# A gated recurrent block with a mixture of experts on one Trainium2 core: rows sorted by expert through DRAM instead of all experts for all rows

## The chip, the cores and the metric

One core of one Trainium2 chip. Its engines work in parallel and meet at semaphores: TensorE (PE; PEld is its weight load), VectorE (DVE), ScalarE (ACT), GpSimd (POOL) and SyncE (SP), which here only issues DMAs. Each engine takes its instructions in program order. The metric is the device time of one execution in microseconds, the median of several runs.

## What is computed

```
x : (32, 128, 256)  ->  batch 32, 128 time steps, 256 features
step t: r = decay*r + c_t*c_t;  inp = (q_t*r) @ Wi.T + bi;  gate = sigmoid(inp @ Wg.T + bg)     # q = layernorm(x), c = ctx
        blended = gate*state + (1-gate)*inp;  state = tanh(blended @ A.T + inp @ Bm.T);  out_t = state @ Wo.T + bo
x = x + tanh(g_xattn) * out
f = layernorm(x)                                       # 4096 rows of 256
shared = swiglu(f @ w_shared_in) @ w_shared_out;  hid = swiglu(f @ w1_shared)
probs = softmax(f @ w_gate + gate_bias)                # 8 experts
routed = sum over the 2 most probable experts e of probs[e] * (hid @ w2[e])
x = x + tanh(g_ffn) * (shared + routed)
```

## The kernel before

**Tiles.** A tile is 8 time steps of the 32 sequences: 256 rows, in two halves of 128. There are 16. A float32 product is made of three fp16 (or fp32r) products of high and low parts: high x high, low x high, high x low. ScalarE makes the high part, GpSimd or VectorE the low one (helper `low`, L1482 on GpSimd).

**The recurrence.** Its 128 steps are a chain: `gated_state` on VectorE forms (1 + gate) x state as u_hi (L1077) and u_lo (L1079, L1082); `recurrence` on TensorE multiplies (8 small matmuls L484, 4 small ones L489) into the tile's accumulator `rec`, which already holds the products that don't depend on the state; `tanh_step` on ScalarE (L777) gives the new state.

**Iterations.** Every engine has a function `iteration(i)`, for i = 1 to 18. Iteration i does the 8 steps of tile i, and between them, as fillers in a fixed order, stages of other tiles: of a = i + 1 the input products (inp, gate, bm, a), of c = i - 1 the output product Wo, second layernorm, w_shared_in, router logits and w1, of d = i - 2 the hidden layers and expert products, of e = i - 3 the last expert products, and of f = i + 2 the first layernorm. Iterations 3 to 12 run in a loop of two; tile 0 and the preparation of weights stand ahead. What stands between step k and k + 1 is called slot k below. Because the engines keep their order, whatever waits in a slot holds the next step up.

**Expert products.** All 8 experts are computed for all rows: `pair(n, m)` multiplies one half of tile m with two experts at once, 6 matmuls of 512 columns (L470):

```python
for kc in range(KC):
    for a, part in ((a_hi, 0), (a_hi, 1), (a_lo, 0)):
        last = pe.matmul(dst, a[:, kc, s * P:(s + 1) * P], w(part, kc), start=first, stop=(kc == KC - 1 and a is a_lo), ...)
```

and `add_pair` on VectorE adds the two results, each times its column of weights `wts` (0 where the expert isn't chosen):

```python
dve.scalar_tensor_tensor(out=o, in0=bank[B_PAIR[n]][:, 0:D], scalar=wts[m % 2][:, s, 2 * q:2 * q + 1], in1=o, op0=ALU.mult, op1=ALU.add)   # L1095
dve.scalar_tensor_tensor(out=o, in0=bank[B_PAIR[n]][:, D:2 * D], scalar=wts[m % 2][:, s, 2 * q + 1:2 * q + 2], in1=o, ...)                  # L1098
```

There are 8 pairs a tile, in slots 0, 1, 2 (of tile e) and 3, 4, 5 (three in slot 5; of tile d). The router's logits come out of TensorE transposed and are turned on VectorE (L1453); which two experts are chosen is found by comparing all with all: `more` and `same` on VectorE (L1352, L1353), five small passes on GpSimd (L1563 to L1580).

**The other fillers of TensorE**: slot 0 transposes of xn1 (L516); slot 1 Wo; slot 2 the shared output product (so); slot 3 inp and gate; slot 4 bm, transposes of xn2 (L528); slot 6 w_shared_in (sh) and logits (L747); slot 7 a and both halves of w1.

**The second layernorm** is a chain through four engines: `projected` (L1167), statistics (L1369 to L1389) on VectorE in slot 2, power and product on GpSimd (L1587, L1589), xn on ScalarE (L860), which stands between the tanh of step 3 and that of step 4; then TensorE transposes. The first layernorm (`x_rstd` on GpSimd, xn1 L849 on ScalarE) stands between the tanh of steps 6 and 7, `residual` (L1498) follows on GpSimd.

**Order of the DMA queue.** SyncE issues per iteration the loads of x, context and the residual's x, and the output of tile i - 3.

## Time and profile before

| | |
|---|---|
| median of 3 runs (531.85 to 532.77) | 532.03 us |
| profiled execution, its own time | 534.36 us |
| its span, first to last instruction | 532.1 us |
| mean granted TensorE clock | 0.973 |
| PE busy | 494.0 us, 93% |
| DVE busy | 436.9 us, 82% |
| ACT busy | 216.6 us, 41% |
| POOL busy | 174.8 us, 33% |

Times below are of that execution, from its span's start. Matmuls are pipelined: "busy" counts each from issue to a modelled end, so how fast TensorE goes is read from distances between starts. The granted clock is a share of full speed, 2.4 GHz.

### The profile page before, as it was taken

How to read it: one execution, taken by the hardware profiler on the slowest of the kernel's cores; microseconds unless marked ns; L12 is line 12 of the kernel's file. 1: busy time of each engine (PE TensorE's matmuls, PEld its weight loads, DVE VectorE, ACT ScalarE, POOL GpSimd, SP SyncE). 2: the span in 40 equal slices, each digit the busy share in tenths (PEclk: the TensorE clock that was granted, in tenths of full speed). 3: DMA queues.
4: the chain of work that ended last, by engine and by line, in shares of the span. 5: the costliest groups of instructions: out<-in, count | busy, mean ns of one | idle time of the engine just before them, and what ended most of it. 6: DMA issues, size and time to landing. Idle time of an engine off the chain costs nothing.

```text
span 532.1 us, 12569 instructions
## 1 busy us (share of the span) xinstructions
PE 494.0 (93%) x4506; PEld 369.6 (69%) x4506; DVE 436.9 (82%) x1382; ACT 216.6 (41%) x500; POOL 174.8 (33%) x261
## 2 busy tenths in 40 slices
PE   5978677999999999999999999999999999979986
PEld 4865566776867776767768777767678687747552
DVE  3788849788898978888898989888888978797976
ACT  4566564443533434434434335344444343322120
POOL 3021564432324233233323243332433243241330
PEclk8999788999999999999999999999999999989999
DMA  6751011020202020110202020301220101000001
GB/s 158 228 165 35 1 36 26 2 61 22 60 22 59 10 69 0 47 32 20 59 20 59 20 59 0 73 5 36 43 59 1 41 1 42 1 20 1 22 1 39
DMA packets 46062, 22.05 MB, mean 41 GB/s; under 512 B 35664, under 2 KB 39376, under 8 KB 46032
## 3 DMA queue, kind: packets, MB, share of 16 engines
q1 hardware_dynamic: 45904, 21.65, 15.8%
q8 instruction: 18, 0.29, 0.2%
q0 software_dynamic: 128, 0.00, 0.1%
q14 instruction: 12, 0.10, 0.1%
HBM read 17.45 MB, written 4.19 MB: 41 GB/s over the span
## 4 chain that ended last, share of the span: by engine, by line
PE 59%; DVE 23%; issue 6%; ACT 5%; POOL 1%; DVEq 0%; ACTq 0%
PE bank L459 22%; PE bank L470 21%; PE rec L459 8%; DVE r L1115 3%; PE rec L484 3%; ACT c L788 3%; DVE x L1167 2%; DVE acc L1095 2%; DVE u_full L1079 2%; PE rec L489 2%; DVE c_turned L1108 2%; DVE u_hi L1077 2%; PE bank L528 1%; PE bank L747 1%; DVE ret L1128 1%
## 5 line engine op out<-in xcount | busy, mean ns | idle before, releaser
L777 ACT ACTIVATE state<-rec 128x64 f32<-128x64 f32 x128 | 36.7, 286 | 177.8 <-PE rec L489 177.5
L470 PE MATMUL bank<-w_hi,hid_hi 128*128 128x512 f16 x256 | 97.8, 382 | 8.8 <-DVE x L1167 5.0
L470 PE MATMUL bank<-w_hi,hid_lo 128*128 128x512 f16 x256 | 97.8, 382 | 0.0
L470 PE MATMUL bank<-w_lo,hid_hi 128*128 128x512 f16 x256 | 97.7, 382 | 0.0
L1077 DVE SCALAR_TENSOR_TENSOR u_hi<-gt,state 128x64 f16<-128x64 f32 x127 | 36.4, 286 | 52.3 <-ACT state L777 52.0
L1098 DVE SCALAR_TENSOR_TENSOR acc<-bank,wts,acc 128x256 f32<-128x256 f32 x128 | 62.0, 484 | 4.5
L1095 DVE SCALAR_TENSOR_TENSOR acc<-bank,wts,acc 128x256 f32<-128x256 f32 x128 | 60.8, 475 | 1.8 <-PE bank L470 1.6
L484 PE MATMUL rec<-u_hi,a_hi 128*128 128x32 f16 x512 | 47.6, 194 | 10.5 <-DVE u_hi L1077 9.6
L484 PEld LDWEIGHTS rec<-u_hi,a_hi 128*128 128x128 f16 x512 | 38.0, 98 | 24.8 <-DVE u_hi L1077 18.5
L1482 POOL TENSOR_TENSOR cn_lo<-cn,cn_hi 128x512 fp32r<-128x512 f32 x14 | 17.9, 1276 | 102.4 <-ACT cn_hi L840 102.4
L470 PEld LDWEIGHTS bank<-w_hi,hid_hi 128*128 128x128 f16 x256 | 25.0, 98 | 33.1 <-DVE x L1167 6.5
L484 PE MATMUL rec<-u_hi,a_lo 128*128 128x32 f16 x512 | 47.3, 193 | 0.0
L470 PEld LDWEIGHTS bank<-w_hi,hid_lo 128*128 128x128 f16 x256 | 25.2, 98 | 30.5 <-issue 0.6
L1079 DVE SCALAR_TENSOR_TENSOR u_full<-gt,state 128x64 f32<-128x64 f32 x127 | 39.7, 312 | 0.0
L470 PEld LDWEIGHTS bank<-w_lo,hid_hi 128*128 128x128 f16 x256 | 25.2, 98 | 20.1 <-issue 0.3
L484 PEld LDWEIGHTS rec<-u_hi,a_lo 128*128 128x128 f16 x512 | 35.1, 98 | 5.7 <-issue 0.3
L1082 DVE TENSOR_TENSOR u_lo<-u_full,u_hi 128x64 f16<-128x64 f32 x127 | 35.3, 278 | 4.4
L1482 POOL TENSOR_TENSOR hs_lo<-hs,hs_hi 128x512 f16<-128x512 f32 x16 | 18.6, 1164 | 60.7 <-ACT hs_hi L961 60.7
L489 PE MATMUL rec<-u_lo,a_hi 128*128 128x32 f16 x512 | 36.3, 194 | 2.3 <-DVE u_lo L1082 1.5
L1482 POOL TENSOR_TENSOR st_lo<-state,st_hi 128x512 f16<-128x512 f32 x16 | 18.6, 1161 | 55.8 <-ACT st_hi L949 55.8
L860 ACT ACTIVATE xn<-x,nr,rs 128x256 f32<-128x256 f32 x32 | 17.5, 594 | 47.0 <-POOL nr L1589 47.0
L459 PE MATMUL bank<-xn_hi,sh_hi 128*128 128x256 f16 x128 | 35.6, 278 | 0.0
(228 smaller groups left out, 1460.9 us busy)
## 6 DMA issues: line engine op xcount, KB each, us to landing
x_sb<-in_x_dram SPq DMA_DIRECT2D x16, 256.0 KB, 3.2
c_sb<-in_ctx_dram SPq DMA_DIRECT2D x64, 64.0 KB, 2.8
xr_sb<-in_x_dram SPq DMA_DIRECT2D x16, 256.0 KB, 3.3
out_dram<-acc SPq DMA_DIRECT2D x16, 256.0 KB, 2.5
raw_w<-in_L_ffn_w_dram SPq DMA_DIRECT2D x8, 256.0 KB, 4.4
raw_sh<-n_L_ffn_w_shared_in_dram SPq DMA_DIRECT2D x1, 512.0 KB, 6.2
raw_w<-in_L_ffn_w_shared_dram SPq DMA_DIRECT2D x1, 512.0 KB, 6.6
raw_Wi<-in_L_xattn_Wi_dram SPq DMA_DIRECT2D x1, 256.0 KB, 3.3
```

The source lines that it names most:

```text
L459: last = pe.matmul(o, w[:, kc, at], a[:, kc, :], start=first, stop=(kc == KC - 1 and w is w_lo), skip_group_check=True)
L470: last = pe.matmul(dst, a[:, kc, s * P:(s + 1) * P], w(part, kc), start=first, stop=(kc == KC - 1 and a is a_lo), skip_group_check=True)
L484: pe.matmul(o[:, oc, :], w[:, kc, oc * P:(oc + 1) * P], u_hi[t % 2][:, kc, :], start=False, stop=False, skip_group_check=True)
L489: last = pe.matmul(o[:, oc, :], a16[0][:, kc, oc * P:(oc + 1) * P], u_lo[t % 2][:, kc, :], start=False, stop=(kc == KC - 1), skip_group_ch ...
L777: act.activation(step_of(state[i % 2], t), step_of(rec[i % 2], t), ACT.Tanh, scale=1.0 / PSCALE).then_inc(st_ready[t], 1)
L860: last = act.activation(xn2[c % 2][:, s, :], x1[c % 2][:, s, :], ACT.Identity, bias=nr2[c % 2][:, s:s + 1], scale=rs2[c % 2][:, s:s + 1])
L1077: dve.scalar_tensor_tensor(out=u_hi[p][:, :, :], in0=gate, scalar=1.0, in1=old, op0=ALU.add, op1=ALU.mult).then_inc(uh_ready[t_next], 1)
L1079: dve.scalar_tensor_tensor(out=u_full[p][:, :, :], in0=gate, scalar=1.0, in1=old, op0=ALU.add, op1=ALU.mult).then_inc(uf_ready, 1)
L1082: dve.tensor_tensor(u_lo[p][:, :, :], u_full[p][:, :, :], u_hi[p][:, :, :], ALU.subtract).then_inc(ul_ready[t_next], 1)
L1095: dve.scalar_tensor_tensor(out=o, in0=bank[B_PAIR[n]][:, 0:D], scalar=wts[m % 2][:, s, 2 * q:2 * q + 1], in1=o, op0=ALU.mult, op1=ALU.add) ...
L1098: dve.scalar_tensor_tensor(out=o, in0=bank[B_PAIR[n]][:, D:2 * D], scalar=wts[m % 2][:, s, 2 * q + 1:2 * q + 2], in1=o, op0=ALU.mult, op1= ...
L1482: pool.tensor_tensor(n, whole, hi, ALU.subtract).then_inc(signal, 1)
```

## The change

Tiles 0 to 14 no longer multiply all experts. They are taken in groups ("chunks") of four, four, four and three tiles. For a group:

1. Each tile's hid goes as rows of 512 fp16 (high and low part) into `hid_rows`, because w1 is now computed with rows on the partitions (`w1_part`; half of w1 moves from slot 7 to slot 0 of the next iteration).
2. VectorE finds the two chosen experts with `max` and `max_index`, and one-hot rows of them. TensorE sums them over the group's rows (`prefix`), VectorE works out from it where each row goes (`places`, `rows`): rows of an expert stand together, each expert from a multiple of 128 on, and a table says which expert a block of 128 rows has.
3. GpSimd scatters the rows to DRAM (`hrows`) by indexed DMAs, 4 a tile of 128 rows each.
4. SyncE reads two blocks at a time back, transposed by the DMA (`turn_rows`), into a ring of four buffers. A group has at most 23 blocks (19 for the last): 12, 12, 12 and 10 "duos".
5. `duo` on TensorE multiplies a duo's blocks, each with its expert, whose number it reads from the table into a register: 12 matmuls of 256 columns. ScalarE copies the result to SBUF, SyncE stores it to DRAM (`yrows`).
6. GpSimd gathers, 4 indexed DMAs a tile, the two result rows of each row, and VectorE adds them with their weights (`combine_first`, `combine_second`) into `acc`, of which there is now one per tile.

Duos stand in slots 2, 4 and 5, one each, from iteration last tile of the group + 4 on: iterations 7 to 15 have three, iteration 16 has nine in slot 5 (after the transposes of tile 15), iteration 17 has the last group's ten in slot 5. Scatters stand in the iterations 5 and 6, 9 and 10, 13 and 14, 16; gathers in 11, 12, 15, 16, 17, 18; combines in 12 to 18. Tile 15 stays dense: its eight pairs come after the last duo. Both DRAM buffers of rows are filled with zeros at the start, by two DMAs that ScalarE issues. The loop is written out. The context's transpose and the scan run for tile i + 2 instead of i + 1. The logits product has 8 small matmuls with rows on the partitions, so that VectorE's four transposes and the comparisons go, with GpSimd's five passes.

The core of the diff (lines that rename semaphores and tiles are left out):

```diff
+CHUNKS = ((0, 4), (4, 4), (8, 4), (12, 3))
+DENSE = 15
+RING = 4
+def blocks_of(q):
+    return 4 * CHUNKS[q][1] + E - 1
...
+            def turn_rows(n):
+                q, j, blocks = duo_chunk(n)
+                if j == 0:
+                    sp.wait_ge(scattered, 16 * 4 * (last_of(q) + 1))
...
+                    sp.wait_ge(duo_done, n - RING + 1)
+                sp.dma_start_transpose(hid_t[n % RING][:, :, 0:blocks * P],
+                                       hrows[q % 2][2 * P * j:2 * P * j + blocks * P, :]).then_inc(ht_in[n % RING], 16)
+            def store_y(n):
...
+                sp.wait_ge(y_ready, n + 1)
+                sp.dma_start(yrows[q % 2][2 * P * j:2 * P * j + blocks * P, :].rearrange("(b p) d -> p b d", p=P),
+                             y_sb[n % RING].rearrange("p (b d) -> p b d", d=D)[:, 0:blocks, :]).then_inc(y_out[n % RING], 16)
...
+                for slot in range(STEPS):
+                    for n in DUOS.get((i, slot), ()):
+                        store_y(n)
+                        if n + RING < duos_before(duo_chunk(n)[0] + 1):
+                            turn_rows(n + RING)
+                for q in range(len(CHUNKS)):
+                    if i == START[q] - 1:
+                        for n in range(RING):
+                            turn_rows(duos_before(q) + n)
...
+            def duo(n, dst):
+                q, j, blocks = duo_chunk(n)
+                pe.wait_ge(ht_in[n % RING], 16 * (n // RING + 1))
+                first = True
+                for b in range(blocks):
+                    at = 2 * j + b
+                    e = pe.value_load(table[q][0:1, at:at + 1], min_val=0, max_val=E - 1)
+                    for kc in range(KC):
+                        for part, half in ((0, 0), (1, 0), (0, 1)):
+                            last = pe.matmul(dst[:, b * D:(b + 1) * D], hid_t[n % RING][:, half * KC + kc, b * P:(b + 1) * P],
+                                             split["w2"][part][:, kc, bass.ds(e, 1), :].rearrange("p a b -> p (a b)"), ...)
+            def prefix(q):
+                n = 2 * CHUNKS[q][1]
+                pe.wait_ge(hot_ready, last_of(q) + 1)
+                for pick in range(2):
+                    pe.matmul(dst[:, 0:n * E], upper[:, :], hots[q][:, :, pick, :], ...)
+                for g in range(n):
+                    for pick in range(2):
+                        last = pe.matmul(dst[:, (g + 1) * E:(n + 1) * E], ones16[:, :], hots[q][:, g, pick, :]..., ...)
...
             def iteration(i, k):     # TensorE
-                    pair(5, e, k)
+                    w1_part(d, D, bank[B_W1B], w1_done, k)
                 recurrence(i, 1, k)
-                    pair(6, e, k)
                 recurrence(i, 2, k)
-                    pair(7, e, k)
+                duos_at(i, 2)
+                for q in range(len(CHUNKS)):
+                    if d == last_of(q):
+                        prefix(q)
                 recurrence(i, 3, k)
-                    pair(0, d, k)
                 recurrence(i, 4, k)
-                    addend_bm(a, k)
-                    pair(1, d, k)
+                duos_at(i, 4)
                     x1_transposed(c, k)
                 recurrence(i, 5, k)
-                    pair(2, d, k)
-                    pair(3, d, k)
-                    pair(4, d, k)
+                    addend_bm(a, k)
+                duos_at(i, 5)
+                if i == DENSE + 2:
+                    for n in range(E):
+                        pair(n)
...
+            for n in range(2):       # ScalarE, setup
+                act.dma_start(hrows[n].rearrange("(b p) d -> p b d", p=P),
+                              zeros[:, :].unsqueeze(1).to_broadcast([P, MOST_BLOCKS, 2 * D])).then_inc(zeroed, 16)
+            def y_evacuated(i, slot):    # ScalarE, after tanh 3, 5 and 6
+                    act.wait_ge(duo_done, n + 1)
+                    act.copy(y_sb[n % RING][:, cols], duo_bank(n, i, slot)[:, cols]).then_inc(y_ready, 1)
...
+            def combine_first(t):
+                dve.wait_ge(gathered[t % 4], 64 * (t // 4 + 1))
+                for s in range(HALVES):
+                    last = dve.scalar_tensor_tensor(out=acc[t][:, s, :], in0=yg[t % 4][:, s, 0, :], scalar=mix[:, t, s, 0:1],
+                                                    in1=acc[t][:, s, :], op0=ALU.mult, op1=ALU.add)
+            def places(q):           # VectorE, slot 4 of iteration last tile + 2; seven small operations
+            def rows(q):             # VectorE, slot 5 of it; six more, the last:
+                dve.tensor_copy(slots_i[q][:, :], slots_f[:, 0:2 * n]).then_inc(routed, 1)
...
+            def scatter(t, s, pick):
+                    pool.wait_ge(routed, 5 * (q + 1))
+                pool.indirect_dma_start(hrows[q % 2], bass.IndirectOffsetOnAxis(ap=slots_i[q][:, at:at + 1], axis=0),
+                                        hid_rows[t % 6][:, s, :, :].rearrange("p a d -> p (a d)"), None, ...).then_inc(scattered, 16)
+            def gather(t, s, pick):
+                    for r in range(RING):
+                        pool.wait_ge(y_out[r], 16 * IN_RING[q][r])
+                    pool.wait_ge(combined, t - 3)
+                pool.indirect_dma_start(yg[t % 4][:, s, pick, :], None, yrows[q % 2], bass.IndirectOffsetOnAxis(...), ...)
+            for q, (t, n) in enumerate(CHUNKS):
+                r = last_of(q) + 2
+                if r < TILES:
+                    spread(SCATTERS, r, range(t, t + 2), [5] * 4 + [7] * 4)
+                    spread(SCATTERS, r + 1, range(t + 2, t + n), range(8))
+                else:
+                    spread(SCATTERS, r, range(t, t + n), [5] * 4 + [6] * 4 + [7] * 4)
...
                 # GpSimd's iteration: moves(i, 0) to moves(i, 7) issue what is planned for (i, spot)
+                moves(i, 0)          # after st_lo
                 low(hs_s[1], ...)
+                moves(i, 1)
                 low(hid_rows[d % 6][:, :, 1, :], ...)
+                moves(i, 2)
                 # second layernorm's power and product
+                moves(i, 3)
+                moves(i, 4)
                     cn_low(a, k)
+                moves(i, 5)
                 x_rstd(f, k)
+                moves(i, 6)
                 residual(i, k)
+                moves(i, 7)
```

## Rows read from the trace of the kernel before

**Rows 1.** Stretches: length, busy us (xcount) of PE, PEld, DVE, ACT, POOL, clock, DMA share.
```profile
0.00:51.86 51.86, 38.97 (x303) 32.95 (x304) 36.14 (x114) 29.02 (x60) 10.43 (x20) 0.90 0.55 150
51.86:81.60 29.74, 22.17 (x216) 18.30 (x215) 20.79 (x65) 17.95 (x38) 16.30 (x18) 0.83 0.13 28
81.60:111.30 29.70, 27.13 (x259) 21.46 (x260) 24.47 (x77) 12.00 (x29) 13.36 (x18) 0.94 0.13 28
...
170.16:434.85 264.69, 260.23 (x2486) 196.29 (x2487) 227.91 (x738) 109.08 (x261) 89.25 (x135) 1.00 0.14 33
...
464.24:487.78 23.54, 20.87 (x190) 13.35 (x189) 18.52 (x60) 5.29 (x15) 6.51 (x11) 0.93 0.03 12
487.78:532.10 44.32, 37.92 (x230) 21.92 (x228) 34.46 (x91) 7.83 (x15) 10.13 (x17) 0.98 0.05 19
```
**Rows 2.** Timeline of ScalarE, the tanh of steps 3 to 6 of one tile.
```profile
237.59 0.29 ACT L777 ACTIVATE state<-rec 128x64 f32<-128x64 f32 x1 [0.77 <-PE rec L489]
...
242.64 0.29 ACT L777 ACTIVATE state<-rec 128x64 f32<-128x64 f32 x1 [0.50 <-PE rec L489]
...
246.25 0.28 ACT L777 ACTIVATE state<-rec 128x64 f32<-128x64 f32 x1 [1.88 <-PE rec L489]
250.48 0.29 ACT L777 ACTIVATE state<-rec 128x64 f32<-128x64 f32 x1 [1.79 <-PE rec L489]
```
**Rows 3.** The chain of waits, 216.8 to 246.3: start, us, what.
```profile
216.81 3.88 PE bank L470 x18
...
221.05 2.62 PE bank L459 x24
...
224.11 0.23 PE rec L484 x8
224.34 0.12 PE rec L489 x4
224.46 1.49 PE rec L459 x12
...
239.42 2.81 PE bank L459 x24
```
**Rows 4.** VectorE by line and form.
```profile
L1095 DVE SCALAR_TENSOR_TENSOR acc<-bank,wts,acc 128x256 f32<-128x256 f32 x128 | 60.8, 475 | 1.8 <-PE bank L470 1.6
...
L1453 DVE STREAM_TRANSPOSE lg_t<-bank 32x64 f32<-32x64 f32 x64 | 15.6, 244 | 2.6 <-PE bank L747 2.0
```
**Rows 5.** Timelines of VectorE and ScalarE: first use of w2, and one layernorm.
```profile
42.60 1.86 DVE L1049 TENSOR_REDUCE w2max<-raw_w 128x1 f32<-128x512 f32 x3
...
236.50 0.26 DVE L1077 SCALAR_TENSOR_TENSOR u_hi<-gt,state 128x64 f16<-128x64 f32 x1
...
239.70 0.16 DVE L1389 TENSOR_SCALAR nm<-mv 128x2 f32<-128x2 f32 x1
...
241.05 1.09 ACT L860 ACTIVATE xn<-x,nr,rs 128x256 f32<-128x256 f32 x2 [3.17 <-POOL nr L1589]
```
**Rows 6.** DMA queues, and issues with KB each and median us to landing.
```profile
q1 hardware_dynamic: 45904, 21.65, 15.8%
...
out_dram<-acc SPq DMA_DIRECT2D x16, 256.0 KB, 2.5
raw_w<-in_L_ffn_w_dram SPq DMA_DIRECT2D x8, 256.0 KB, 4.4
...
raw_so<-_L_ffn_w_shared_out_dram SPq DMA_DIRECT2D x1, 256.0 KB, 6.9
...
cols<-in_L_xattn_bi_dram POOLq DMA_DIRECT2D x1, 1.0 KB, 2.9
```
**Rows 7.** GpSimd by line: a DMA that it issues.
```profile
L1515 POOL DMA_DIRECT2D cols<-in_L_xattn_bi_dram x1 | 0.8, 781 | 0.0
```
**Rows 8.** The tail: ScalarE's timeline, and the chain of waits.
```profile
497.67 1.09 ACT L860 ACTIVATE xn<-x,nr,rs 128x256 f32<-128x256 f32 x2 [3.06 <-POOL nr L1589]
...
518.95 9.25 PE bank L470 x42
```

More of the change, by code:

```diff
@@ new lines, in duo_slots, with put @@
+        def duo_slots():
+            plan = {}
+            def put(i, slot, n):
+                plan.setdefault((i, slot), []).extend(n)
+            for q in range(len(CHUNKS)):
+                n = list(range(duos_before(q), duos_before(q + 1)))
+                i = last_of(q) + 4
+                while n and i < TILES:
+                    for slot in (2, 4, 5):
+                        put(i, slot, n[:1])
+                        n = n[1:]
+                    i += 1
+                if n:
+                    put(TILES + (q == len(CHUNKS) - 1), 5, n)
+            return plan
@@ new lines, in rows @@
+            def rows(q):
+                n, base, step = 2 * CHUNKS[q][1], 7 * q, 5 * q
+                blocks = blocks_of(q)
+                dve.wait_ge(routing, base + 7)
+                for pick in range(2):
+                    last = dve.tensor_tensor(placed[:, 0:n, pick, :], hots[q][:, :, pick, :], place[:, 0:n, :], ALU.mult)
+                last.then_inc(routed, 1)
+                dve.tensor_reduce(counted[:, 0:blocks], reached[:, 0:blocks, :], AX_X, ALU.add).then_inc(routed, 1)
+                dve.wait_ge(routed, step + 1)
+                dve.tensor_reduce(slots_f[:, 0:2 * n], placed[:, 0:n, :, :].rearrange("p g k e -> p (g k) e"), AX_X,
+                                  ALU.add).then_inc(routed, 1)
+                dve.wait_ge(routed, step + 2)
+                dve.tensor_scalar(table[q][:, :], counted[:, 0:blocks], float(E - 1), None, ALU.min).then_inc(routed, 1)
+                dve.wait_ge(routed, step + 3)
+                dve.tensor_copy(slots_i[q][:, :], slots_f[:, 0:2 * n]).then_inc(routed, 1)
@@ L1540, in iteration, with moves @@
+            for i, tiles in GATHER.items():
+                spread(GATHERS, i, tiles, list(range(8)) if i < TILES else [0, 0, 1, 1, 2, 2, 3, 3] if i == TILES else [5] * 16)
+            def moves(i, spot):
+                for t, s, pick in SCATTERS.get((i, spot), ()):
+                    scatter(t, s, pick)
+                for t, s, pick in GATHERS.get((i, spot), ()):
+                    gather(t, s, pick)
             def iteration(i, k):
```

638 lines of the change are left out of this document (389 added, 249 removed).

## The prediction

> **What bounds the kernel now.** I read four views. The table by stretches [rows 1] divides the span. The recurrence ends at 487.78: 51.86 us of setup and tile 0, 29.7 us each for tiles 1 and 2, 29.4 us for each tile from 3 to 14, 23.5 us for tile 15, then a tail of 44.3 us. In the middle stretch (nine tiles, 264.69 us) TensorE is busy for 260.23 us, VectorE for 227.91, GpSimd for 89.25, at granted clock 1.00, the 2.4 GHz level. The chain of waits [rows 3] shows TensorE going from one filler to the next: between two steps of the recurrence (8 + 4 small matmuls, 0.23 + 0.12 us) lie 18 expert matmuls of 512 columns (3.88 us, so 0.216 each) or 24 of 256 columns (2.62, so 0.109 each). The tanh rows [rows 2] agree: 246.25 to 250.48 is 4.23 us = 3.88 + 0.35. So a step lasts as long as TensorE's filler in its slot plus 0.35, unless a chain across the engines is longer. One is: 237.59 to 242.64 is 5.05 us, which fillers alone don't make. There ScalarE waits for the second layernorm [rows 5]: 3.17 us idle ahead of xn.
>
> **What is removed.** A tile has 8 pairs x 6 matmuls x 0.216 = 10.4 us of expert work on TensorE, all of it in filler slots, and 16 accumulations of 0.475 us on VectorE (7.6 us) [rows 3, 4]. Both go for tiles 0 to 14.
>
> **What is left, slot by slot, without duos (iterations 3 to 6).** Slot k is what lies between steps k and k + 1. TensorE's filler: transposes 0.44 + half of w1 (12 x 0.109 = 1.31); wo 1.31; so 1.31; inp and gate 24 in 2.8; transposes 0.44; bm 1.5 (12 of fp32r); sh and the now small gate product 2.9; a and the other half of w1 2.8 [rows 3]. With 0.35 each they sum to 17.7 us. VectorE needs 25.3 - 7.6 - 1.0 (four small transposes), plus some 1.2 for max, max_index and one-hot rows, so about 18 us. No engine fills a tile alone, so the longest in each slot counts, and I get 2.2, 2.3 (VectorE), 2.1 (VectorE), 4.3, 1.8, 2.4, 3.5, 3.15. The 4.3 is the layernorm chain: from u_hi at 236.50 to xn's end at 242.14 are 5.64 us, of which some 0.2 for the softmax's small rows leave; the tanh is 1.09 after u_hi, and the next tanh is queued behind xn on ScalarE [rows 2, 5]. The 2.4 and 3.5 are ScalarE waiting for blend, and for GpSimd's statistics. Sum 21.75; the same method gives 28.3 for the tile before, against 29.4, so I add 0.6 for waits it doesn't see: **22.3 us, 7.1 less**, four times: 28. Tile 2 (five pairs leave, 6.5 us) gives 7.
>
> **Duos.** A duo is 12 matmuls of 256 columns, 1.31 us, plus two reads of an expert number from SBUF into a register of TensorE and an address worked out from it. No row shows such a read. Between 0 (hidden under the six matmuls before, 0.65) and 1.1 us each (the layernorm's whole pair of ScalarE operations takes 1.09 [rows 5], nothing small costs more) I take 0.4: 2.1 us. Slots 2, 4 and 5 get one each. Slot 2 grows to 3.8, but what follows then isn't the layernorm chain any more (3.15 for inp and gate), slot 4 to 2.8, slot 5 to 3.9, slot 6 falls to 3.25. Sum 24.5, with waits 25: **4.4 less**, eight times (7 to 14): 35. In tile 15 (23.54 before) three pairs of slots keep their size and the duos replace pairs: 19.5, 4 less.
>
> The Trainium skill (DMA: Bandwidth & Descriptors, Latency and other measured facts) gives a register load of about 600 ns as its floor; by it an exposed duo would be 2.5 us and the nine tiles some 10 us longer in all, if each read were exposed. No row here shows it.
>
> **What the sorting adds to the tiles.** Sixty scatters and sixty gathers are issued on GpSimd. Its plain small DMAs take 0.78 us [rows 7]; an indexed one must read 128 offsets too, so the lower end is 0.78, the upper twice that, 1.6, and I take 1.1, between them. One alone between two passes is hidden by GpSimd's idle time (it is busy 9.9 of 29.4 us a tile). Four in one place are not: in iterations 5, 9 and 13 four scatters stand ahead of x_rstd and wait for the routing table, which comes 1.7 us after step 6; xn1 is 4.4 + 0.9 + 1.09 later, and tanh 7 is queued behind xn1 on ScalarE. That is 4.6 us in iteration 5 and 3.3 in 9 and 13; the thirteen dependent small operations of `places` and `rows` on VectorE add 2 in 5, nothing in the others (TensorE's duo covers them), and the queue behind adds about 1 each: 16 us in all. The first duo of a group (7, 11, 15) waits for the last scatter, a landing and a transpose, about 2 us each: 6. Combines on VectorE stand in slot 7 of 12 to 15: 3.4 us. **Sum 25.** Zeroing writes 2 x 2944 rows of 1 KB, 6.0 MB. The queue's 21.65 MB took 15.8% of 532 us [rows 6], so 23 us of all engines, beside the weight loads. Those of w2, the last, land in 4.4 and are first used at 42.6 [rows 5, 6], and in the first 51.86 us the engines' share is only 0.55 [rows 1], so I take the weights as in time; I count 2 us for two DMA issues in ScalarE's full setup, less 1 for the four transposes. If weights come late it is up to 12.
> What moves without a price: scan and context transpose run a tile further ahead, which only lengthens their slack; the loop of the middle tiles is written out, and neither its border nor code loading shows in the 29.4 us before. SyncE waits for the last scatter of a group in iterations 6, 10, 14 and 16; behind it are queued the next loads of x and context, used one to two tiles later, and xr, used a tile later, so at a landing of 4.4 us [rows 6] they stay covered.
> The recurrence then ends at 487.8 + 1 - 7 - 28 - 35 - 4 + 25 = **440**, so 48 us earlier.
>
> **The tail, counted from there (T).** Before it is 44.3. Now 19 duos of two groups and the dense tile remain. Layernorm and transposes of tile 15: before, xn ends at T + 11 [rows 8]; eight gathers (6.6 of them ahead of it) put it at T + 14. Nine duos at 2.1: T + 33. Shared, router and w1 products 5.5, hid and its halves 2.5: T + 41. Ten duos: T + 62. Behind them eight dense pairs, 10.4 us (42 matmuls took 9.25 [rows 8]): T + 72, at the half clock more. Longer is the other way: last duo, copy and store (0.6, 0.5 to issue, 2.5 to land [rows 6]) T + 65.6; twelve gathers 13.2; landing 2.9 [rows 6]; last combine 1.9; output 2.5: **T + 86**, 42 us more than before. A duo is read through a ring of four: its loop is copy 0.6 + issue 0.5 + landing + duo 2.1, and four duos take 8.4; so it is hidden as long as a transposing DMA lands within 5.2 us. The same 256 KB untransposed lands in 4.4 (median) to 6.9 [rows 6]. I take 4.4 to 5.
>
> Against this stands a page. The Trainium skill (VectorE: DVE Perf Modes, The three transpose paths) gives 1309 ns for a 128x128 two-byte transpose by DMA; a duo holds eight of these, and added up they would be an estimated 10.5 us. That rule speaks against the change; as a mechanism of this kernel it is the second rival. No row here shows a transposing DMA.
>
> **Sum.** 440 + 86 = 526 us of span; the profiled run has 2.3 us around its span of 532.1 (534.36 in all), so 528 against 534.4, or 1.2% less. Against the median 532.03 this is **526 us**.
>
> **Rivals.**
> *Cheaper parts* (0.22): indexed DMAs at 0.78 and duos at 1.6. Tiles: 27 duos x 0.5, 12 scatters x 0.3 and 3 us at the starts of groups, 20 less; tail: 19 duos x 0.3 (the ring then holds them at 1.8) and 12 gathers x 0.3, 9 less: 497 us. For it: the DMA row [rows 7] and the queue of TensorE that runs ahead. Against: each duo has addresses to work out.
> *Slow transposes* (0.22, ends slower): one place, the ring of four. With L from a transposing DMA's issue to its landing, a loop of four duos takes L + 3.2 us once L is above 5.2. Nine duos are two loops and a duo, ten are a first L, two loops and two duos, and the first duo of three groups in the tiles waits L as well. So each us of L above 5.2 costs 2 + 3 + 3 = 8 us: at L = 7 14 more, 540; at L = 10 38 more, 564. It decides from L = 5.9 on. For it: two-byte elements must be placed across partitions, and plain landings go to 6.9 already [rows 6]. Against: the middle of them lies at 4.4, on queues fuller than the tail's. (By the page's 10.5 us the time would be an estimated 568.)
> *Dear indexed DMAs* (0.14, ends slower): at 1.6 us each 0.5 x 12 in the last gathers, 0.5 x 12 in the stalls of 5, 9 and 13, some 3 us at the starts of groups, and the last group's scatters end after its ring is free (4 us): 19 more, 545. It decides from 1.3 us on.
> *Nothing gained in the tiles*: the forecast of 22.3 rests on chains; if all tiles stayed at 29.4 the tail would make it 574. The freed 10.4 us of the engine that bounds speak against it (it shares the 0.14).
>
> **Chances and range.** My forecast, the tiles gain 48 and the tail gives back 42, has 0.42. It is a small difference of two large terms, each off by 5 us easily, so its own range is 515 to 538, of which 0.33 lies below 531, 0.03 within 0.2% of 532 (about what a measurement tells from no change) and 0.06 above. Faster is 0.33 + 0.22 = 0.55, slower 0.06 + 0.22 + 0.14 = 0.42, the same 0.03. A tenth on either side is left out by 492 to 564.
>
> **What would show it.** In the profile after: tanh 0 to tanh 0 of iterations 3 and 4 at 22 us and of 8 or 12 at 25, TensorE's share about 80%; the longest single wait of tanh before step 7 of 5, 9, 13, released by GpSimd; the recurrence's end at 440; the rows of indexed DMAs on GpSimd near 1.1 us; the transposes' landing under 5.2; a tail of 86 us whose chain ends in gathers and combines. It is wrong if those DMAs cost another size, if the clock falls to 1.2 GHz in the tail's gaps, or if the weights are late in the setup.

## The result and the profile after

The changed kernel takes **578.73 us** (median of 4 runs, 576.92 to 582.35) against 532.17 for the kernel before beside it: 1.0875 times as long, 95% interval 1.0834 to 1.0916. I had said 526, with 492 to 564. It is slower, and outside the range. A run that takes over 1.5% more than the shortest run of the same kernel is left out of its median; only e8 below has such runs, two of four.

The profiled run took 576.92 us around a span of 575.04. The same cuts as in [rows 1], by tanh 0 of iterations 1, 2, 3 and 15 and by the last tanh (length, then busy us and count of TensorE, its weight loads, VectorE, ScalarE, GpSimd, then granted clock, DMA share, GB/s):

```profile
0.00:59.14 59.14, 42.24 (x303) 35.73 (x304) 36.95 (x108) 29.09 (x59) 11.15 (x24) 0.91 0.82 238
59.14:88.46 29.32, 19.33 (x209) 15.78 (x209) 20.06 (x65) 18.95 (x40) 16.61 (x17) 0.94 0.07 15
88.46:113.04 24.58, 19.62 (x235) 17.20 (x236) 21.04 (x67) 11.57 (x31) 12.32 (x13) 1.00 0.11 28
113.04:436.35 323.31, 271.32 (x3119) 238.74 (x3118) 244.98 (x842) 149.23 (x367) 171.60 (x182) 0.95 0.38 91
436.35:460.06 23.71, 16.84 (x192) 12.92 (x190) 14.88 (x57) 6.42 (x17) 13.71 (x15) 0.93 0.82 183
460.06:575.04 114.98, 61.55 (x398) 36.93 (x396) 45.30 (x132) 18.03 (x34) 55.22 (x55) 0.79 0.60 158
```

Against before: setup and the first two iterations 88.46 - 81.60 = 6.9 us longer; tiles 2 to 15 take 371.6 in place of 406.2, so 34.6 shorter; the tail takes 115.0 in place of 44.3, so 70.7 longer. Sum +43, which is the difference of the spans (575.0 - 532.1). TensorE's share falls from the 98% of the middle stretch before to 84% here and 54% in the tail: it no longer sets the pace. The granted clock shows the same: 96.5 us of the span at the 1.2 GHz level, 28.8 before, and half of the 96.5 (48.7) lie in the tail.

The other rows of the page and the list of waits that answer to [rows 6, 7]: queues and GpSimd's groups, then what ScalarE's layernorms waited for (total us, times, longest).

```profile
q1 hardware_dynamic: 104432, 44.73, 32.8%
q0 software_dynamic: 5888, 15.74, 9.5%
q10 hardware_dynamic: 5920, 6.03, 3.0%
...
L1818 POOL DMA_INDIRECT yg<-yrows,slots_i x60 | 62.0, 1033 | 32.1 <-issue 16.1
L1805 POOL DMA_INDIRECT hrows<-hid_rows,slots_i x60 | 62.8, 1047 | 21.8 <-issue 18.1
```
```profile
ACT xn L1002 <- POOL nr L1747: 58.5, 15, 9.7
ACT xn L1013 <- POOL nr L1880: 46.7, 16, 8.6
```

An indexed DMA holds GpSimd for 1.04 us, as forecast (1.1), but 0.30 us of "issue" stands between two of them: their pitch is 1.30. GpSimd's timeline in iteration 5, where the longest of these waits lies:

```profile
184.09 0.97 POOL L1805 DMA_INDIRECT hrows<-hid_rows,slots_i  x1 [0.30 <-issue]
185.37 0.97 POOL L1805 DMA_INDIRECT hrows<-hid_rows,slots_i  x1 [0.30 <-issue]
186.36 0.74 POOL L1745 TENSOR_TENSOR rs<-ve,minus_half 128x2 f32<-128x2 f32 x1
187.18 0.19 POOL L1747 TENSOR_TENSOR nr<-nm,rs 128x2 f32<-128x2 f32 x1
187.32 1.41 POOL L1754 TENSOR_TENSOR xr_sb<-xr_sb,tgbo 128x256 f32<-128x256 f32 x2
188.89 1.07 POOL L1805 DMA_INDIRECT hrows<-hid_rows,slots_i  x1 [0.16 <-issue]
...
192.82 0.97 POOL L1805 DMA_INDIRECT hrows<-hid_rows,slots_i  x1 [0.30 <-issue]
193.81 1.17 POOL L1738 TENSOR_TENSOR st_lo<-state,st_hi 128x512 f16<-128x512 f32 x1
195.15 1.00 POOL L1805 DMA_INDIRECT hrows<-hid_rows,slots_i  x1 [0.17 <-issue]
196.17 1.17 POOL L1738 TENSOR_TENSOR hs_lo<-hs,hs_hi 128x512 f16<-128x512 f32 x1
```

Two small operations (rs, nr) stand behind the scatters, then come four more scatters, and only at 193.81 the state's low part, whose input from ScalarE was ready at 189.7. The next low part, hs_lo, stands behind one more scatter. Both delays end in ScalarE's queue. Its tanh starts give the slots of iterations 5 and 6: 2.1, 3.0, 1.5, 5.4, 1.6, 3.7, **11.0**, 1.6 and **5.1**, 3.1, 2.2, 5.0, 1.5, 2.5, 5.1, 2.6.

The tail from the last tanh (T = 460.06): nine duos from T + 15.6 to T + 43.3, ten from T + 51.4 to T + 87.6, end T + 115. TensorE inside the nine (timeline; "issue" is a wait that no semaphore explains):

```profile
484.59 0.28 PE L614 MATMUL bank<-w_hi,raw_w 128*128 x1 [0.45 <-issue]
...
487.78 0.28 PE L614 MATMUL rec<-w_hi,raw_w 128*128 x1 [0.92 <-issue]
...
489.12 0.37 PE L614 MATMUL rec<-w_lo,raw_w 128*128 x1 [0.46 <-issue]
...
491.33 0.39 PE L614 MATMUL rec<-w_hi,raw_sh 128*128 x1 [1.63 <-issue]
491.94 0.37 PE L614 MATMUL rec<-w_lo,raw_sh 128*128 x1 [0.22 <-issue]
...
493.38 0.37 PE L614 MATMUL rec<-w_lo,raw_sh 128*128 x1 [0.30 <-issue]
...
496.21 0.39 PE L614 MATMUL rec<-w_hi,raw_sh 128*128 x1 [2.25 <-issue]
```

A block of six matmuls takes 0.83 us in an even stretch, and the next follows 0.3 to 0.6 later. From 487 to 497 the longer gaps are 0.9 to 2.3 us, and they lie inside blocks too. The same comes back from 522 to 543. GpSimd issues twelve scatters from 478.8 to 494 and sixteen gathers from 515.6 to 537.

TensorE's results are also taken late. The last matmul of the fourth duo starts at 485.15, and ScalarE's copy of that duo, which waits for it, starts 8.2 us later ("remote" is a release that the view can't name):

```profile
485.15 0.27 PE L614 MATMUL bank<-w_hi,raw_w 128*128 x1
493.32 0.59 ACT L1107 COPY squares_w<-bank 128x512 f32<-128x512 f32 x1 [10.09 <-remote]
```

In an even stretch the copy follows 0.3 us behind its duo's last matmul. Four of the nineteen copies of the tail come late like this: 8.2 and 7.0 us in the nine duos, 11.4 and 12.8 in the ten. With plain DMAs (e2) or none (e8) all but the first of a stretch come within 0.5, and the first within 1.1.

### The profile page after: what moved, and what is told of

Same layout as the page of the kernel before. It is cut to its first block, busy times and chain, and to the rows that moved or that the text cites. A ratio compares the mean times of both kernels' runs of the same rounds, so it can differ in the third digit from the quotient of the medians.

```text
span 575.0 us, 12774 instructions
## 1 busy us (share of the span) xinstructions
PE 430.9 (75%) x4446; PEld 357.3 (62%) x4446; DVE 383.2 (67%) x1268; ACT 233.3 (41%) x546; POOL 280.6 (49%) x305
## 4 chain that ended last, share of the span: by engine, by line
PE 26%; issue 25%; POOL 20%; DVE 19%; ACT 6%; DMA 2%; POOLq 1%; SPq 1%; DVEq 0%; ACTq 0%
PE bank L562 8%; POOL hrows L1805 6%; POOL yg L1818 5%; PE rec L614 4%; PE bank L614 4%; PE bank L573 3%; DVE u_hi L1250 3%; DVE ret_lo L1210 2%; PE rec L562 2%; DVE u_full L1252 2%; POOL hid_rows L1738 2%; PE rec L587 1%; DVE u_lo L1255 1%; POOL rs L1745 1%; ACT c L941 1%
## 5 line engine op out<-in xcount | busy, mean ns | idle before, releaser
L1250 DVE SCALAR_TENSOR_TENSOR u_hi<-gt,state 128x64 f16<-128x64 f32 x127 | 49.6, 391 | 90.1 <-ACT state L930 80.3
L1818 POOL DMA_INDIRECT yg<-yrows,slots_i x60 | 62.0, 1033 | 32.1 <-issue 16.1
L1805 POOL DMA_INDIRECT hrows<-hid_rows,slots_i x60 | 62.8, 1047 | 21.8 <-issue 18.1
L587 PE MATMUL rec<-u_hi,a_lo 128*128 128x32 f16 x512 | 48.7, 196 | 0.0
L1738 POOL TENSOR_TENSOR hid_rows<-hid,hid_rows 128x512 f16<-128x512 f32 x15 | 19.9, 1324 | 49.0 <-ACT hid_rows L1152 49.0
L562 PE MATMUL bank<-xn_hi,sh_hi 128*128 128x256 f16 x128 | 36.2, 283 | 7.9 <-DVE xn_lo L1660 7.9
L1002 ACT ACTIVATE xn<-x_sb,nr,rs 128x256 f32<-128x256 f32 x32 | 17.5, 593 | 58.5 <-POOL nr L1747 58.5
L562 PE MATMUL bank<-xn_lo,sh_hi 128*128 128x256 f16 x128 | 36.3, 284 | 0.0
L562 PE MATMUL bank<-xn_hi,sh_lo 128*128 128x256 f16 x128 | 36.3, 283 | 0.0
L573 PE MATMUL bank<-w_hi,xn_hi 128*128 128x256 f16 x120 | 35.2, 293 | 0.0
L573 PE MATMUL bank<-w_lo,xn_hi 128*128 128x256 f16 x120 | 35.0, 292 | 0.0
L562 PE MATMUL bank<-ret_hi,inp_hi 128*128 128x256 f32 x64 | 21.7, 338 | 17.8 <-DVE ret_lo L1210 17.7
L573 PE MATMUL bank<-w_hi,xn_lo 128*128 128x256 f16 x120 | 34.9, 291 | 0.0
```

The source lines that it names most:

```text
L562: last = pe.matmul(o, w[:, kc, at], a[:, kc, :], start=first, stop=(kc == KC - 1 and w is w_lo), skip_group_check=True)
L587: pe.matmul(o[:, oc, :], w[:, kc, oc * P:(oc + 1) * P], u_hi[t % 2][:, kc, :], start=False, stop=False, skip_group_check=True)
L1250: dve.scalar_tensor_tensor(out=u_hi[p][:, :, :], in0=gate, scalar=1.0, in1=old, op0=ALU.add, op1=ALU.mult).then_inc(uh_ready, 1)
L1738: pool.tensor_tensor(n, whole, hi, ALU.subtract).then_inc(signal, 1)
L1805: pool.indirect_dma_start(hrows[q % 2], bass.IndirectOffsetOnAxis(ap=slots_i[q][:, at:at + 1], axis=0), hid_rows[t % 6][:, s, :, :].rearra ...
L1818: pool.indirect_dma_start(yg[t % 4][:, s, pick, :], None, yrows[q % 2], bass.IndirectOffsetOnAxis(ap=slots_i[q][:, at:at + 1], axis=0), bo ...
```

## The experiments

All times are medians of at least four runs (e8: of two), with the span of one profiled. The theory that I started from: the price lies in the indexed DMAs and in what a duo has around its matmuls. The rivals: transposes and their ring, the register loads alone, the zero fill, the unrolled code, and a tail that is long because of its amount of work.

**e1, a fixed expert for each block.**
```
- e = pe.value_load(table[q][0:1, at:at + 1], ...)
+ e = at % E
```


> Leaves out the reading of the block's expert: block number modulo 8 is taken, so that the product has no register load and no address worked out at run time; 46 duos with the same matmuls stay. In the changed kernel the tail after the last tanh is 115 us. In it 17 register instructions of TensorE's queue last 0.6 to 1.4 us each, in two stretches (487 to 497 and 522 to 539 us) that cost about 7 and 14 us against the usual pace, and elsewhere a duo comes every 2.5 us though its matmuls take 1.5. Theory A (the register instructions are what is dear, usual and stalled alike): both stretches go and a tail duo comes every 1.6 to 1.8 us; tail 80 to 90 us, time 540 to 553. Rival B (TensorE's instructions of any kind come late in those stretches): 0.8 us for each of 19 tail duos goes, the two stretches stay: tail 100, time 562 to 568. Rival C (the landing of the ring's transposed rows sets the pace of the tail): under 5 us goes, time above 573. Tiles 2 to 15 change by under 3 us by each of them, as the blocks there have gaps of 0 to 0.4 us.


Measured 565.29 (562.7 to 567.25), 13.4 us less, the recurrence's end at 462.0, tail 103.1: rival B's time. A duo in an even stretch fell from 2.4 to 1.31 us, so the reads cost 0.55 each where nothing covers them, more than B had. And both stretches stayed, in part as waits for the ring: the nine duos take 22.7 us, the ten 29.6, where the matmuls alone would need 11 and 12. One such wait in this run's timeline of TensorE:
```profile
517.58 0.27 PE L614 MATMUL rec<-w_hi,raw_sh 128*128 128x256 f16 x1 [3.12 <-DMA raw_sh<-hrows]
```
So register instructions aren't the only ones that are late in the stretches.

**e2, plain DMAs in place of the indexed ones.**
```
- pool.indirect_dma_start(hrows[q % 2], IndirectOffsetOnAxis(slots_i...), hid_rows...)
+ pool.dma_start(hrows[q % 2][at * P:(at + 1) * P, :], hid_rows...)     (gathers alike)
```


> Leaves out the sorting: each of the 120 indexed DMAs of GpSimd becomes a plain DMA of GpSimd with the same bytes to or from 128 fixed consecutive rows; queues, waits and order stay. Theory A (a run of indexed DMAs, back to back on GpSimd, is what makes TensorE's register instructions wait 0.7 us each at 487 to 497 and 522 to 539 us): the two stretches go, 15 to 21 us less, and the cheaper issue (0.8 + 0.3 against 1.0 + 0.3 us) takes 0.2 us from each of some 36 DMAs that the end waits for, 5 us more: time 550 to 558. Rival B (the stretches come from TensorE's own supply of instructions, whatever GpSimd does): they stay, time 570 to 575. Rival C (every DMA of GpSimd does it, indexed or plain): they stay or get shorter by a third, time 565 to 572.


Measured 535.25 (532.59 to 536.44): 43 us less, far more than the 21 to 29 of theory A. Its page:
```profile
L1816 POOL DMA_DIRECT2D yg<-yrows x60 | 32.9, 552 | 27.4 <-DMA yrows<-squares_sh 25.1
...
L1805 POOL DMA_DIRECT2D hrows<-hid_rows x60 | 33.1, 555 | 7.4 <-issue 4.0
```
A plain DMA of 128 KB has a pitch of 0.53 us (back to back from 450.0 to 455.3), an indexed one 1.30. 24.3 us go in tiles 2 to 15 (347.3 against 371.6) and 17 in the tail (98.0); the setup is 1 shorter. None of the three theories had this: all had looked at the tail alone.

**e3, plain loads in place of the transposing DMAs.**
```
- sp.dma_start_transpose(hid_t[n % RING][...], hrows[q % 2][...])
+ sp.dma_start(hid_t[n % RING]..., hrows[q % 2][...].rearrange("(p a) d -> p (a d)", p=P))
```


> Leaves out the transposition: each of the 46 transposing DMAs of SyncE (issue 1.2 to 1.7 us) becomes a plain load of the same bytes, 2 KB a partition; the duos multiply rows that aren't turned. Theory A (slow transposes in SyncE's queue and on the DMA engines set the tail's pace, my rival in the prediction): the four that stand between the last scatter and the first of the ten duos cost 3 us less, and the ring gives a duo every 2.5 us: 12 to 18 us less, 561 to 567. Rival B (TensorE's queue sets the pace; the rows have landed by then): under 5 us less, 574 to 579. In the setup and in tiles 2 to 15 under 3 us by both.


Measured 576.08 (574.64 to 579.75), within 3 us of the changed kernel: rival B. So the transposing itself isn't what is slow.

**e4 and e6, the zero fill later**, on ScalarE in iteration 3, then on SyncE in iteration 2.
```
- act: for n in range(2): act.dma_start(hrows[n]..., zeros...)       in the setup
+ e4: the same in ScalarE's iteration 3      e6: sp.dma_start(...) in SyncE's iteration 2
```


> Moves the two DMAs that fill the row buffers in DRAM with zeros (6.03 MB) from the setup to iteration 3; nothing is left out. The setup was 6.4 us longer than before the change, where I had predicted 1. Theory A (the zero fill holds up the loads of weights, context and x in the setup): setup 5 to 7 us shorter, iteration 3 within 1 us: time 571.5 to 574. Rival B (the setup is longer for other reasons: prefix constants, the new router, the unrolled code): within 1.5 us of the changed kernel, 577 to 580.

> Moves the two DMAs of the zero fill from ScalarE's queue in the setup to SyncE's queue in iteration 2. Nothing is left out. The last run moved them to ScalarE in iteration 3: the setup got 6.4 us shorter and slot 0 of iteration 3 5.7 us longer, as the second of the two issues held ScalarE for 6.1 us (8.2 us in the setup). Theory A (the price is the second issue on a full queue, paid by the engine that issues it, and SyncE has time): setup 6.4 us shorter, iterations 2 and 3 as before within 1 us, time 571 to 573.5. Rival B (the 6 MB of packets delay others wherever they are issued): 576 to 580.


e4 measured 578.49 (577.42 to 580.68), nothing gained. The first tanh comes at 27.5 again, as before the change, and not at 33.9; but tanh 1 of iteration 3 comes 5.7 us late. ScalarE's timeline there:
```profile
107.98 0.29 ACT L930 ACTIVATE state<-rec 128x64 f32<-128x64 f32 x1 [1.34 <-PE rec L592]
108.01 6.56 ACTq L1118 DMA_DIRECT2D hrows<-zeros  x2
114.67 0.69 ACT L1126 ACTIVATE sil_w<-bank,in_un 128x512 f32<-128x512 f32 x1 [6.40 <-issue]
```
Of the two issues the first took 0.43 us and the second 6.1: it holds the engine that issues it. By its time e4 is rival B's, but the 6 us of the setup did go and came back in iteration 3. In e6 SyncE is held for 6.4 us, with nothing urgent behind it: 575.18 (570.84 to 577.82), 3.5 less, in the direction of theory A. The intervals of the two ratios (1.0726 to 1.0852, 1.0834 to 1.0916) overlap a little, so the size isn't settled.

**e5, the four early scatters behind x_rstd.**
```
- spread(SCATTERS, r, range(t, t + 2), [5] * 4 + [7] * 4)
+ spread(SCATTERS, r, range(t, t + 2), [6] * 4 + [7] * 4)
```


> Moves the four scatters that stand ahead of x_rstd in GpSimd's queue, in iterations 5, 9 and 13, behind it (ahead of residual). Nothing is left out. Slot 6 of those iterations took 10.0 to 11.0 us in the changed kernel, where x_normalised waits up to 9.7 us for x_rstd's result; slot 6 takes 4.3 us in iterations 2 to 4. Theory A (the wait for x_rstd is the whole cost): three times 5.5 to 6.5 us go, time 559 to 562. Rival B (GpSimd itself is late: eight scatters at 1.3 us still stand ahead of the state's low part of the next iteration, so the wait moves to its slots 0 and 1): under 5 us of the 18 goes, 573 to 577.


Measured 580.74 (577.16 to 582.29): nothing is gained, rival B's mechanism, above its 573 to 577. Slot 6 of iterations 5, 9, 13 falls from 11.0, 10.0, 10.1 to 6.8, 4.3, 4.3 us, and slot 1 of 6, 10, 14 rises from 3.1, 3.1, 3.0 to 6.8, 8.9, 8.8. The wait moves: this other order gains nothing, because the eight scatters take GpSimd's time either way.

**e7, gathers of tiles 8 to 11 with pauses.**
```
+ if q == 2:
+     pool.wait_ge(duo_done, duos_before(3) + 1 + at // 2)
```


> The 16 gathers of tiles 8 to 11 in the tail no longer follow one another without a pause: each pair of them waits for one more of the ten duos to be finished. Nothing is left out. In the changed kernel they run from 515.6 to 537 us and TensorE stutters from 522 to 543. Theory A (an unbroken run of indexed DMAs is what makes TensorE's instructions and the ring's transposes late): the ten duos take 26 to 29 us in place of 36, time 568 to 572. Rival B (each indexed DMA costs the same, spread or not): the duos take 34 to 37 us and the last gathers start no earlier: 576 to 581.


Measured 572.11 (567.3 to 573.05), 6.6 less: theory A by the ten duos, at the edge of its time. The table by stretches, nine and ten duos, first of the changed kernel, then of e7:
```profile
475.67:503.40 27.73, 17.91 (x105) 10.36 (x105) 1.50 (x7) 5.28 (x9) 12.51 (x13) 0.76 0.68 176
511.46:547.70 36.24, 19.71 (x117) 10.77 (x115) 15.84 (x48) 5.80 (x11) 17.68 (x17) 0.76 0.70 173
```
```profile
477.97:506.00 28.03, 18.68 (x105) 11.31 (x105) 1.50 (x7) 5.17 (x9) 12.51 (x13) 0.75 0.66 174
514.10:542.00 27.90, 19.39 (x116) 11.24 (x114) 13.99 (x44) 5.30 (x10) 17.55 (x17) 0.82 0.99 222
```
The nine, whose scatters weren't touched, still take 28.0; the ten fall from 36.2 to 27.9, with the same sixteen gathers beside them.

**e8, no scatters and gathers at all.**
```
- for t, s, pick in SCATTERS...: scatter(t, s, pick)      (GATHERS alike; also the waits for them)
+ for n in range(4): pool.memset(yg[n]..., 0.0)            (setup: zeros for the combines)
```


> Leaves out all 120 scatters and gathers (rows that were never scattered are turned and multiplied, and the combines add rows of zeros); the zero fill, transposes, duos, y stores and combines stay. GpSimd is left with its old work. Theory A (the moves cost what they hold up: with them gone a tile takes 23 to 24 us as I had reckoned, the nine duos 20 as in the run with the last group dense, the ten duos 22 to 26, and the 16 us of last gathers go): recurrence ends at 420 to 428 us, tail 72 to 80, time 495 to 508. Rival B (transposes, ring and register loads keep their share of the loss): recurrence above 435 or tail above 90, time above 520.


Measured 506.0, the median of 504.45 and 507.59 (left out are 513.05 and 513.81): theory A. Clearing the buffers for the combines takes GpSimd 3.6 us of the setup; the first tanh comes 5.0 us later than in the changed kernel and tanh 0 of iteration 2 6.9 (95.33 against 88.46). The profile is of the run of 513.05, so its stretches are rather too long than too short. Recurrence and tail in it end just above A's 420 to 428 and 72 to 80. Tiles 2 to 15 and the tail, in the table by stretches:
```profile
95.33:428.92 333.59, 300.80 (x3540) 268.09 (x3541) 275.71 (x965) 168.16 (x414) 123.14 (x137) 0.97 0.33 74
428.92:511.30 82.38, 54.62 (x398) 35.27 (x396) 44.07 (x132) 18.11 (x34) 6.71 (x7) 0.94 0.57 146
```
and the nine and the ten duos in it:
```profile
438.85:459.70 20.85, 15.45 (x104) 9.80 (x105) 1.50 (x7) 5.05 (x9) 0.00 (x0) 0.92 0.62 145
467.78:491.20 23.42, 15.73 (x117) 9.87 (x115) 15.47 (x48) 5.89 (x11) 1.15 (x1) 1.00 0.73 177
```
Without the moves a tile takes 23.8 us, tile 15 17.1, and the clock is at 1.00 in the ten duos. Transposes are undisturbed here (count, median us to landing):
```profile
raw_sh<-hrows SPq DMA_TRANSPOSE x24, 3.7
raw_w<-hrows SPq DMA_TRANSPOSE x22, 3.7
```

**e9, the kernel before, unrolled alone.**
```
- with eng.Fori(FIRST_FULL // 2, LAST_FULL // 2) as reg: ...
+ for i in range(1, TILES + 3): iteration(i, Static())
```


> The kernel before with its loop over iterations 3 to 12 written out, one part of the change alone. Nothing is left out. Theory A (unrolling costs and gives nothing: the looped iterations take the same 29.7 us as the written-out iteration 2): 530.5 to 533.5 us. Rival B (register arithmetic in the waits costs the looped kernel 0.5 us or more an iteration): 522 to 528. Rival C (supply of instructions): 536 or more.


Measured 532.96 (530.9 to 534.12), ratio 1.0012 (0.9988 to 1.0035): theory A. Unrolling costs nothing here.

**e10, tiles 12 to 15 dense in the tail.**
```
- CHUNKS = ((0, 4), (4, 4), (8, 4), (12, 3)); DENSE = 15
+ CHUNKS = ((0, 4), (4, 4), (8, 4)); DENSE = 12       # pairs of 12 to 15 behind the nine duos
```


> Tiles 12 to 15 are computed dense, as 32 pairs in the tail, in the place of the last routed group (10 duos, 12 scatters, 12 gathers) and of the one dense tile; tiles 0 to 11 stay routed. Nothing is left out. The changed kernel's tail is 115 us. Theory A (the tail is long through what is put round the matmuls: scatter, transpose, ring, register loads, store, gather): the nine duos end at 36 to 43 us after the last tanh, the products of tile 15 take 8, 32 pairs of 1.28 us take 41, the last combine and store 5: tail 90 to 97, time 552 to 559. Rival B (dense work is what makes a tail long: 32 pairs take more than 60 us as their banks come free late): tail above 110, time above 572.


Measured 573.99 (573.53 to 575.6), tail 107: by the time rival B, though its reason is another. The ratio's interval (1.075 to 1.0847) just overlaps that of the changed kernel, so the 4.7 us less aren't settled. The nine duos are as theory A has them. With twelve scatters gone the nine duos take 20.4 us:
```profile
465.14:480.75 15.61, 6.95 (x52) 5.15 (x51) 8.68 (x35) 4.33 (x9) 11.86 (x13) 0.73 0.37 89
480.75:501.12 20.37, 14.78 (x104) 9.33 (x104) 0.69 (x1) 5.28 (x9) 0.67 (x1) 0.96 0.68 162
```
but the pairs start at T + 49.6 and take 53 us, not 41. They start together with the sixteen gathers of tiles 8 to 11, which GpSimd issues from 514.0 to 534.7. VectorE, which adds the pairs up, waits in this time for TensorE's results:
```profile
527.86 0.48 DVE L1267 SCALAR_TENSOR_TENSOR raw_w<-bank,wts,raw_w 128x256 f32<-128x256 f32 x1 [2.56 <-PE bank L575]
532.12 0.48 DVE L1267 SCALAR_TENSOR_TENSOR raw_w<-bank,wts,raw_w 128x256 f32<-128x256 f32 x1 [3.25 <-PE bank L575]
537.07 0.48 DVE L1267 SCALAR_TENSOR_TENSOR raw_w<-bank,wts,raw_w 128x256 f32<-128x256 f32 x1 [3.94 <-PE bank L575]
```
TensorE's record shows the matmuls of these three pairs done long before: the last ones start at 523.6, 524.9 and 526.2. VectorE waits for pairs 12.7 us in all, about what is missing (53 - 41). So matmuls without any register instruction are taken late beside a run of gathers too. The combines of tiles 8 to 11, from 547.3 on, wait for nothing.

**e11, dense group, zero fill by SyncE and scatters behind x_rstd together.**


> Three edits together, nothing left out: tiles 12 to 15 dense in the tail, zero fill by SyncE in iteration 2, and the four early scatters behind x_rstd. Alone they gave 574.0, 575.2 and 580.7 us against 578. Theory A (they add up, the last giving nothing as GpSimd is busy anyway): 565 to 572. Rival B (with fewer scatters at the end the moved ones have room and give 3 us each): 560 to 565. By neither does it reach the 532 of before.


Measured 564.02 (559.61 to 565.99), ratio 1.0541 (1.0478 to 1.0605): 14.7 less than the changed kernel, where the three alone gave 4.7, 3.5 and -2.0: more than their sum, within rival B's range. Which of the three gives more beside the others wasn't tested. This is the fastest version that leaves nothing out, and it is still 5% slower than the kernel before.

**e13, plain scatters, indexed gathers.** The edit is the first line of e2's.


> Leaves out the sorting on the way in alone: the 60 scatters become plain DMAs of GpSimd of the same bytes to fixed rows; the 60 gathers stay indexed. With both plain the time fell by 43 us, 25 of them ahead of the last tanh. Theory A (the scatters stand in the way of x_rstd and of the state's low part, the gathers mostly beside other work until the tail): 22 to 27 us go, with the stutter of the nine duos and 15 to 20 us of the tiles; time 551 to 556. Rival B (both cost alike): about 20 to 22 us go, 10 to 13 us of them in the tiles: 556 to 559. Rival C (the gathers, of which 28 run in the tail, are the dearer): under 15 us go, above 563.


Measured 557.07 (555.41 to 560.09), 21.7 us less, rival B's time: tiles 2 to 15 take 354.3 (17.3 less, of the 24.3 in e2) and the nine duos 23.9; the ten stutter as before (36.1). Scatters and gathers share the price about equally, the scatters mostly in the tiles, the gathers mostly in the tail (making these plain too takes another 7.0 from the tiles and 13.5 from the tail, e13 against e2).

## Why the prediction was wrong, by its own steps

**What bounds, what leaves, slot by slot: right.** Iteration 3 took 22.9 us for the 22.3 that I had, and its slots 2.1, 3.0, 1.5, 5.4, 1.5, 2.5, 4.3, 2.6 for 2.2, 2.3, 2.1, 4.3, 1.8, 2.4, 3.5, 3.15. The sum is good, the layernorm chain of slot 3 a microsecond short. Iteration 4 took 24.3, with 3.4 us at the 1.2 GHz level inside its slot 3 (6.8). The rival that nothing is gained in the tiles is out.

**Duos: right in kind, the read mis-sized.** 0.55 us for each exposed read in place of 0.4, so 2.3 to 2.4 for a duo in place of 2.1 (e8, e10). In the tiles most are covered by the six matmuls ahead of them; without moves iterations 7 to 14 take 24.0 on average for my 25, and tile 15 17.1 for 19.5. The Trainium skill (DMA: Bandwidth & Descriptors, Latency and other measured facts) puts a register load at about 600 ns at least. The load itself is 0.30 us in the record here (median of 88); with the address and the restart 0.55 are lost, so the estimate of 2.5 for a duo by the page would have been nearer.

**Sorting in the tiles: this step failed, with the overlap that it took for granted.** I had 16 us for the stalls at the scatters of 5, 9 and 13, 6 for the first duos, and nothing for a move that stands "alone between two passes", since GpSimd was busy for only 9.9 of 29.4 us. With and without moves (changed kernel less e8), iterations 5, 9 and 13 differ by 4.0 + 4.8 + 7.8 = 16.6 us (7, 8 and the first three cancel to -0.3): that term is right. But iterations 6, 10, 11, 12, 14 and 15, with mostly one move ahead of each pass, differ by 2.6 + 5.0 + 3.0 + 2.2 + 2.3 + 6.6 = 21.7. In all the moves cost 38.0 us of the tiles where I had 22. GpSimd's passes are short, but rs, nr and the low parts stand one behind another in the chains that set the slots, and each waits for the rest of a 1.3 us DMA. An idle share says nothing about that. Some 6 of the 21.7 us are another thing, the late results of TensorE described above: in slot 4 of iteration 15 (5.5 us, 2.6 in e8) the last small matmul of the step starts at 449.83 and its tanh at 453.34, beside four gathers in a row, and nothing of GpSimd's work stands between them. Before the change, in e2 and in e8 no tanh is late like this. e2 tells that it is the time on GpSimd: at a pitch of 0.53 iterations 6, 10, 11 and 12 cost 1.3 us above e8 each, at 1.30 they cost 3.2. e5 tells that its reordering inside the iteration doesn't help. (e8's profile has more of its early tiles at the 1.2 GHz level and is 1.4 us longer in slot 3 of iterations 2 and 3, so the 38.0 is rather low.)

**Setup: mis-sized.** I had +1, it is +6.9 at tanh 0 of iteration 2. The term of 2 us for two DMA issues on ScalarE was 8.6 us: the second one blocked the engine for 8.2. With them gone from ScalarE's setup tanh 0 of iteration 2 comes at 83.1 (e6).

**The tail: start and middle right, but the ring of duos was priced as if nothing ran beside it, and this step failed.** Nine duos start at T + 15.6 (my T + 14), the products between the groups take 8.1 (8), and what follows the last duo 27.3 (24). The duos themselves take 27.7 and 36.2 where I had 19 and 21, 24 us more. Four of these are the dearer read (20.8 and 23.4 in e8). The other 20 come with GpSimd's DMAs running one after another beside them. It is shown two ways: in the nine duos they go when the scatters go (e10: 20.4), and about half of them when these are plain (e13: 23.9 of 27.7); of the ten duos' 12.8 us, 8.3 go with pauses between the gathers (e7: 27.9). e1 agrees, where both stretches stay without a register load, though there the ring is drawn on faster and its own pace may be part of it. Plain gathers don't spare the ten duos (34.1 in e2): there they come more than twice as densely, and it is the ring's transposes that land late. That the clock might fall to 1.2 GHz in the tail's gaps was on my list; its mean is 0.79 there, and 48.7 us of the tail are at that level. It explains only some 4 of the 20: 55 distances between two matmuls of a tail duo are about 0.21 us in place of 0.11, against 18 in e8, while the distances of 1 us and more sum to 20.1 us, against 1.1 in e8.

**The rivals.** *Slow transposes* were to decide from a landing of 5.9 us. They land in 3.7 undisturbed (e8; the changed kernel's trace gives no landing for them), and making them plain gives under 3 us (e3). The Trainium skill (VectorE: DVE Perf Modes, The three transpose paths) gives 1309 ns for one 128x128 two-byte transpose; the estimate of 10.5 us for a duo's eight, one after another, isn't what e8's trace has, 3.7 for all eight. *Dear indexed DMAs* was the right suspect with too small a price: at 1.3 us each, its own threshold, it makes some 8 of its 19 us, 534, because it counted each DMA for the time by which it is longer where four stand in a row. The full price of the 120 moves is what e8 leaves out: 578.7 - 506.0, and 7 more for the setup of e8, some 80 us or 0.66 us each; the two profiles, of the shortest run here and a long one there, differ by 38.0 in the tiles and 32.6 in the tail, 70.6. *Cheaper parts* is out. *Nothing gained in the tiles* had 574, near the 578.7, by luck: the tiles did gain 34.6.

**The account.** From my span of 526 to the 575.0: setup 5.9, tiles 14.2, tail 29.0. In the tiles the moves are 16 above my sum, and the rest 2 below it.

**What stays open.** Which shared part they wait for isn't shown. Two kinds of things are late. One is TensorE's register instructions: in the two stretches of the tail ten that work out or check an expert's address, and wait for no semaphore, last 0.66 to 1.39 us, against some hundredths elsewhere (median 0.05 for the commonest); in e2 and e8 none of them lasts over 0.5. The other is what an engine is told of TensorE's finished matmuls (ScalarE's copies, a tanh, VectorE's pairs in e10). A rival that no run excludes is the recording itself: of the semaphore updates of the DMAs (16 each in the kernel before) this trace lacks 1583 of 5616, the traces of the kernel before, of e2 and of e8 lack none, and every trace with indexed DMAs lacks some. The recording may only suffer from the same crowd, or it may be what holds the engines.

## What to carry to other kernels

Price a DMA that GpSimd issues by its pitch, and then ask which small GpSimd operations of a latency chain stand behind it: each of them can be late by the rest of it, whatever GpSimd's idle share. Taking the pairs out of the tiles was worth 72.6 us in the tiles (406.2 - 333.6); moving the rows there and back by 120 indexed DMAs of 128 rows took 38 of these back. The tail, where nothing is left to hide the routed chain, grew by 70.7, twice what the tiles had gained. Computing the last group densely gave 4.7 us here (e10), and 14.7 together with two other edits (e11), so it doesn't save the change; ending the routed part several tiles earlier wasn't tried.
